# An adaLN block with experts on one core: the order of the gated down products, and where a quarter of the one-hot rows is made

## The reference, cut to what matters

```python
scores = sigmoid(h @ gate_w.T)                      # 4096 tokens, 16 experts
topk_score, topk_ids = top_k(scores.T, cap)         # cap = 512 tokens for each expert
xin = h[topk_ids]
up = einsum('ecd,efd->ecf', xin, up_w) + up_b       # f = 1024
g = einsum('ecd,efd->ecf', xin, gw) + gb
eo = silu(g) * up
eo = einsum('ecf,edf->ecd', eo, down_w) + down_b    # d = 256
flat = eo * topk_score[..., None]
out = zeros_like(h).at[topk_ids].add(flat) + shared
```

## Time and profile before

| what | value |
|---|---|
| median of 3 runs | 1221.22 us (1215.82, 1221.22, 1225.65) |
| profiled execution | 1223.39 us, its span 1221.7 us |
| granted clock over the span | 0.96 of full speed |
| first and last start of a down product's matmul | 470.6 us and 1212.6 us (in the shared layer and in expert 15) |
| down products of expert 0 begin | 652.23 us |
| first to last HTl | 448.7 to 1202.9 us |

### The profile page before, as it was taken

One profiled execution on the slowest core, in us unless ns is written; L12 is line 12 of the kernel. 1 busy time (PEld: TensorE's weight loads), 2 busy tenths in 40 slices (PEclk: granted clock), 3 DMA queues, 4 the chain that ended last, 5 costly groups with the idle time before them and its releaser, 6 DMA issues.

```text
span 1221.7 us, 21693 instructions
## 1 busy us (share of the span) xinstructions
PE 1130.8 (93%) x7481; PEld 878.8 (72%) x7482; DVE 862.9 (71%) x2197; ACT 600.4 (49%) x1085; POOL 628.9 (51%) x670
## 2 busy tenths in 40 slices
PE   8888989898899988999888999999999999999997
PEld 4545646555555567887677888888888888888886
DVE  4587888797887547778667776677776677776562
ACT  2257777766775644221244454444454444454441
POOL 4124476575674642222335656655656655666654
PEclk8689999999999898999999999999999999999999
DMA  6736677978878444874245445554445554446531
GB/s 185 87 59 116 106 124 166 181 125 165 146 141 163 149 160 159 244 205 133 75 155 133 120 133 146 137 133 121 135 126 155 128 134 119 141 124 160 126 87 18
DMA packets 100589, 165.47 MB, mean 135 GB/s; under 512 B 18680, under 2 KB 65272, under 8 KB 98432
## 3 DMA queue, kind: packets, MB, share of 16 engines
q1 hardware_dynamic: 83616, 137.07, 45.1%
q0 software_dynamic: 14336, 25.70, 10.9%
q10 hardware_dynamic: 2528, 1.32, 0.9%
HBM read 103.97 MB, written 34.13 MB: 113 GB/s over the span
## 4 chain that ended last, share of the span: by engine, by line
PE 33%; POOL 23%; issue 17%; DMA 10%; DVE 10%; SPq 3%; ACT 3%; ACTq 1%; POOLq 0%; DVEq 0%
POOL HTl L1744 12%; PE LB L804 6%; PE MB L804 6%; PE MB L513 4%; POOL out_y L1784 4%; PE LB L513 4%; POOL XG L1751 4%; DMA HT<-Us 3%; DVE junk L1221 3%; PE UB L513 2%; SPq L310 2%; PE UB L635 2%; PE XB L513 2%; PE LB L612 2%; DMA XT<-hD 2%
## 5 line engine op out<-in xcount | busy, mean ns | idle before, releaser
L1744 POOL TENSOR_TENSOR HTl<-HF,HTh 128x512 fp32r<-128x512 f32 x160 | 222.0, 1393 | 252.2 <-ACT HTh L1016 251.9
L1221 DVE CUSTOM_DVE_ANT_0 junk<-MB,MK 128x256 bf16<-128x256 f32 (+3 forms) x512 | 219.8, 483 | 60.1 <-PE MB L583 58.8
L1654 POOL TENSOR_SCALAR_AFFINE_SELECT P<-P 128x256 f32<-128x256 f32 x256 | 101.4, 420 | 145.4 <-ACT P L956 145.4
L1016 ACT ACTIVATE HTh<-HF 128x512 fp32r<-128x512 f32 x160 | 100.4, 627 | 91.1 <-DVE HF L1532 91.1
L1784 POOL DMA_INDIRECT out_y<-EO,IDX x64 | 106.7, 1666 | 69.2 <-DVE EO L1617 63.7
L583 PE MATMUL MB<-KS,QS 48*128 48x256 f32 (+3 forms) x512 | 131.3, 368 | 8.3 <-DVE NM L1221 4.3
L954 ACT ACTIVATE P<-LB 128x768 f32<-128x768 f32 x124 | 100.6, 812 | 70.3 <-PE LB L612 70.0
L1023 ACT ACTIVATE SIL<-LB,gbT 128x512 f32<-128x512 f32 x64 | 43.9, 685 | 185.4 <-PE LB L513 185.3
L612 PE MATMUL LB<-QS,KS 50*128 50x256 f32 x496 | 120.4, 360 | 10.6 <-ACT P L954 8.2
L612 PEld LDWEIGHTS LB<-QS,KS 50*128 50x128 f32 x496 | 77.1, 193 | 56.1 <-issue 41.0
L804 PE MATMUL LB<-WDh,HTh 128*128 128x256 f32 x320 | 94.0, 294 | 18.0 <-POOL HTl L1744 18.0
(11 more groups left out here) (281 smaller groups left out, 3040.3 us busy)
## 6 DMA issues: line engine op xcount, KB each, us to landing
WR<-in_gw SPq DMA_DIRECT2D x16, 1024.0 KB, 7.2
WR<-in_uw SPq DMA_DIRECT2D x16, 1024.0 KB, 4.9
WR<-in_dw SPq DMA_DIRECT2D x16, 1024.0 KB, 5.5
QS<-ST SPq DMA_DIRECT2D x96, 128.0 KB, 5.1
KS<-ST SPq DMA_DIRECT2D x90, 128.0 KB, 6.0
hD<-h SPq DMA_DIRECT2D x8, 1024.0 KB, 5.5
XT<-hD SPq DMA_DIRECT2D x8, 1024.0 KB, 8.7
X<-in_x SPq DMA_DIRECT2D x8, 512.0 KB, 6.5
```

Source lines behind the costliest of these rows:

```text
L1221: m = e.tensor_tensor_reduce(junk[:, o:o + w], MB[:, o:o + w], MK[:, 512 - w:512], 1.0, -3e38, ALU.add, ALU.max, NM[:, k // 4, 4 * (k % 4) ...
L1654: m = e.affine_select(out=dd, in_=dd, compare_op=ALU.is_ge, fill=0.0, base=0, pattern=[[0, 2], [1, 128]], channel_multiplier=-1)
L1744: e.tensor_tensor(HTl[:, slot, :], HF[i][:], HTh[:, slot, :].bitcast(F32), ALU.subtract).then_inc(g_ht, 1)
```

## The change

It changes the order of two queues. On TensorE the first two down products of an expert were issued as blocks 0 to 6 of the first, 0 to 3 of the second, 7 of the first, 4 to 7 of the second. They become blocks 0 to 5 of the first, 0 to 5 of the second, then 6 and 7 of the first and 6 and 7 of the second. On VectorE the fourth quarter of the one-hot rows moves from step 5 to the stage of the down products, behind the second `tb`, EO and cut. Nothing is added or removed, and the last two products are as before.

```diff
             slots, g0, d0 = list(range(8)), n_eglu(x_, 0) - 1, n_edown(x_, 0) - 1
-            down(d0, 0, slots, g0, range(7), piece_d(x_))
-            down(d0 + 1, 1, slots, g0, range(4))
-            down(d0, 0, slots, g0, (7,))
-            down(d0 + 1, 1, slots, g0, (4, 5, 6, 7))
+
+            down(d0, 0, slots, g0, range(6), piece_d(x_))
+            down(d0 + 1, 1, slots, g0, range(6))
+            down(d0, 0, slots, g0, (6, 7), piece_d(x_))
+            down(d0 + 1, 1, slots, g0, (6, 7))
             down(d0 + 2, 2, slots, g0, range(8))
             down(d0 + 3, 3, slots, g0, range(8))
...
-                if x_ + 2 < NE and 2 <= m_ < 6:
+                if x_ + 2 < NE and 2 <= m_ < 5:
                     onehot(x_ + 2, m_ - 2)
...
                 if nxt:
                     cut(e, piece_u(x_ + 1), q)
+                if x_ + 2 < NE and q == 1:
+                    onehot(x_ + 2, 3)
```

## The result

The changed kernel took 1206.12 us (median of 4 runs, 1200.49 to 1208.30); the kernel before, with one more run, 1219.99 us. Forecast were 1204.8 us and a ratio of 0.9866. The profiled executions are 1223.39 us before and 1204.28 us after, 19.1 us apart, and their traces say which part of this is the change.

What follows compares the result with a forecast made beforehand. TensorE, busy 93% of the span, was taken as the bound, stalled by late HTl. Stall 17.2 us off, new wait 0.8 on: 16.4 off the 1221.22 us median gives 1204.8; own range 1200 to 1209.5, 8-in-10 range 1199 to 1213.

Steps and rivals of the forecast that it cites:

- The stall and its place: Down products, experts 0 to 13: PE waits on HTl, late because the fourth one-hot quarter precedes HF of slot 6.
- The size, 17.2 us off: Down stage: the stall costs 1.23 us against expert 14 and goes altogether in 14 experts, 17.2 us off.
- rival (b): Gated steps: another chain takes the pace, TensorE stalling later on gathers, weights or HF; 1221 us, chance 0.12.
- HTl of slot 7 at T0 + 3.0: GpSimd's HTl of slot 7 ends 3.0 us after the down products start (T0), instead of T0 + 5.10.
- rival (a): VectorE pieces and HTl hold each other up, slot 7 stays late, 7 us of gain lost: 1212 us, chance 0.12.
- Either part would do most of it: Down stage: moving the quarter or reordering blocks would alone remove most of the stall; the two gains don't add.
- The new wait, 0.05 us x 16: Third down product waits for VectorE's read of the first accumulator, fewer blocks between: 0.8 us on over 16 experts.
- The landing place, price 0: Quarter behind the second cut makes the third read 0.4 us late without holding PE; without that cover, 5.6 us.
- The sum: Whole kernel: 17.2 - 0.8 = 16.4 us off; profiled execution 1207.0 us, median 1204.8 us, 1.3% less.

Runs made afterwards that it cites:

- order-only run: Against the changed kernel, the fourth one-hot quarter stays in step 5, new block order kept: 1215.48 us, ratio to the kernel before 0.9950, period 36.14 us.
- one block less between: Against the changed kernel, one block of the second product instead of two before the third product: 1215.02 us, ratio to before 0.9929, period 36.03 us.
- pair-in-step-2 kernels: Against the changed kernel, one-hot quarters 0 and 1 both in step 2, none in step 3: 1206.11 us with old block order, 1206.49 with new.
- kernel with all quarters late: Against the changed kernel, old block order and all four one-hot quarters in the down stage, one behind each cut: 1202.82 us, period 35.42 us.
- first series: First of two series of runs, on two chips; in it the unchanged kernel before took 1221.85 us (29 runs), the changed kernel 1209.86.

## Why the prediction was right

**The stall and its place.** All 14 waits of PE on HTl are gone in the changed kernel. Leaving the quarter in step 5 brings the lateness back (HTl of slot 7 at T0 + 5.08 in the order-only run, 5.10 before); moving it alone removes it. That the quarter made HTl late is shown.

**The size, 17.2 us off.** The stage fell by 12.82 - 11.65 = 1.17 us, that is 1.23 for the stall less 0.06 for the new wait. Taking expert 14 of the same trace as the picture of the other 14 without their stall was good to 0.01 us: with only the quarter moved the stage takes the same 11.59 to 11.60 us in all of them. Nothing behind the stage gave the gain back (rival (b)): the gated steps take 23.94 and 24.1 us in odd and even experts of both kernels.

**HTl of slot 7 at T0 + 3.0.** It was 3.34. The HF of slot 6 came exactly the 2.2 us earlier, but the cut behind it took 1.13 us, not 0.68, since HTl of slot 5 (861.32, 1.46) ran beside it. I had taken that cut's length from a stretch where no HTl ran. This was rival (a)'s mechanism, and it took 0.3 of the 1.8 us to spare; PE asked at T0 + 4.76. But that rival names the XT as of the same kind, and the rows don't bear that out. XT's subtraction reads one of its two inputs from an accumulator (XB). At 863.25 it took 0.68 us with an HTl beside it from 863.42 on, and that HTl took 1.31: neither was held up.

**Either part would do most of it.** Half wrong. The quarter alone does all (35.61 us). The order alone does 0.69 of 1.17 us, and the prediction had worked out only the quarter's case, although the numbers of the other stood in its rival (a), 5.10 against 4.8: 0.5 us left in each of the experts that wait.

**The new wait, 0.05 us x 16.** 0.06 in the stage, 0.05 between the periods of the two orders, and 0.37 with one block less between. Expert 14 of the changed kernel has it as well (1148.59 to 1160.23, 11.64 us, against 11.59). The rule of the Trainium skill (TensorE: Matmul & The Clock Gate, section "Wait — 56ns, not 53.3ns?") gives a beat of 109 ns as an estimate, and from it 0.13 us for this wait. Neither is what this kernel does: the trace after stays at 0.12 us too.

**The landing place, price 0.** The third read came 0.41 us late (872.68; the product's last matmul starts at 871.95, so it was due at 872.27), as worked out, and the fourth on time. But the sentence that the quarter costs nothing beside scatters looked at one side only. The second scatter took 1.90 us where the other three of this expert took 1.55 to 1.75: it started at 872.30, with the quarter running until 872.77. The slack hid it there; in the pair-in-step-2 kernels the same effect on a gather cost most of the gain (35.56 against 35.42 us).

**The sum.** 1204.8 was forecast, 1206.12 measured, inside the scatter; on the traces 16.4 us were forecast and 16.4 are between the marks. The closeness of the whole times is partly luck: the profiled execution was forecast at 1207.0 and took 1204.28, and that gap is nearly all the 2.9 us ahead of the first mark, for which the prediction has no term.

## What to carry to other kernels

When only some iterations of a loop have a stall, compare the same stage in an iteration that has none: here that gave the price to a hundredth, and what the iteration lacks names the suspect. Look at two neighbouring iterations before taking a price for all: here odd and even ones differed. Look for the work that stands in the wrong queue ahead of a late operand before covering its lateness with another order on the bound engine; here the cover was worth half and cost a little, the move was worth all. And when small work moves to idle time, ask on both engines who is running there: in these rows the one that started second paid.

## What the runs showed that I had not expected

A one-hot quarter delays GpSimd's instruction for an indirect transfer that starts while the quarter runs: 1.96 instead of 0.98 us for a gather (started 883.00, quarters until 884.13), 1.90 instead of some 1.6 for a scatter. It is no single case. In the kernel with all quarters late, 51 scatters start with 0.7 to 0.9 us of a quarter still to run; they take 2.13 to 2.44 us and end 1.4 to 1.5 us after it. One that had started first is not delayed, nor is the quarter behind it: 1.02 and 1.22 us. The Trainium skill (SBUF — State Buffer, section "Who interferes with whom") reports a probe in which a VectorE tensor_tensor did not stall a transfer, and infers a reason; these rows disagree.

Expert 0 is reached at very different times: the first mark lies between 645.19 and 653.55 us in ten profiled executions, 8 us, while the 14 periods behind it repeat within 0.01 us each where the order is the same. The kernels differ ahead of that mark only in the quarters of expert 0, and the changed kernel alone, run three times, has it at 646.39, 648.99 and 649.64. The granted clock may have to do with it. Over the 29 runs of the kernel before in the first series, time and the run's granted clock go together (1212.00 us at 0.968, 1229.79 at 0.950; correlation -0.88). The marks follow the clock only loosely: up to 640 us it is 0.92 in the first repeat of the changed kernel with the mark at 649.64, and 0.93 in the kernel before with the mark at 651.88. No run held the clock fixed, so a cause isn't shown.

The beat of the large matmuls goes with the experts' parity. The mean from start to start is 0.228 us in the gated steps of odd experts, which use the second set of buffers for weights and tokens, and 0.232 in those of even experts with the first set, in all ten traces and at a granted clock of 1.00. Over the 96 matmuls of the gated steps that makes 0.4 us, and 0.42 is what odd and even experts differ by in the table above where no quarter is left. In the other kernels the wait in step 6 costs the odd experts, with the faster beat, some five times as much as the even ones, and so neighbouring periods differ by only about 0.15 us (the last transposes of experts 5 to 8 of the changed kernel start at 827.23, 862.95, 898.53 and 934.26). Why one set is slower is open.
